# First attention of a fused eight-layer kernel: a head's query and key weights absorbed two heads ahead instead of one

## The reference, cut to what matters

```python
q = rmsnorm(x @ Wq_a) @ Wq_b             # rank 192, then per head 128 plain + 64 rotary columns
ckv = x @ Wkv_a                          # 64 compressed + 64 rotary columns
kv = rmsnorm(ckv[..., :64]) @ Wkv_b      # per head 128 key + 128 value columns
scores = (q_nope @ k_nope.T + rope(q_pe) @ rope(k_pe).T) * 192 ** -0.5
probs = softmax(where(causal, scores, -inf))
out = concat_heads(probs @ v) @ Wo
```

## Time and profile before

| what | us |
|---|---|
| median of 3 runs | 3092.81 |
| lowest, highest run | 3090.31, 3095.83 |
| profiled execution: its span | 3095.1 |
| profiled execution: its own time outside the span | not given |
| PE busy in the span | 2679.5 (87%) |
| DVE, ACT, POOL busy | 1575.6, 1260.3, 650.4 |
| the first attention's heads | from about 60 to 1127 |

### The profile page before, as it was taken

The page is one execution under the profiler, slowest core; times in us unless marked ns, Lnnn a source line. Parts: engine busy times, 40 slices in busy tenths (PEclk is TensorE's granted clock), DMA queues, the critical chain, the costliest instruction groups (busy, mean ns, idle before and its releaser), DMA issues. The chain is left out here.

```text
span 3095.1 us, 37611 instructions
## 1 busy us (share of the span) xinstructions
PE 2679.5 (87%) x12992; PEld 1314.1 (42%) x12992; DVE 1575.6 (51%) x2697; ACT 1260.3 (41%) x1756; POOL 650.4 (21%) x506
## 2 busy tenths in 40 slices
PE   4999999999999989664999997568999998799766
PEld 3455555555555557222333332322333333344344
DVE  3444544545445434456777774526777773111343
ACT  3344444444444432220666566222565665100321
POOL 0344444444444430230000001210000001000121
PEclk7798898998989889886999998789999999899878
DMA  2010110100111021021000000141011000300001
GB/s 61 13 36 26 31 37 26 36 26 26 36 33 34 22 72 62 20 76 49 14 14 21 20 1 15 41 106 37 22 25 39 22 1 14 110 0 0 16 0 51
DMA packets 72234, 99.82 MB, mean 32 GB/s; under 512 B 34536, under 2 KB 42984, under 8 KB 69824
## 3 DMA queue, kind: packets, MB, share of 16 engines
q1 hardware_dynamic: 72128, 98.31, 11.2%
HBM read 77.17 MB, written 20.84 MB: 32 GB/s over the span
## 5 line engine op out<-in xcount | busy, mean ns | idle before, releaser
L1935 POOL TENSOR_TENSOR l0a_p_low<-yT,l0a_p_high 128x1024 fp32r<-128x1024 f32 (+7 forms) x256 | 396.4, 1554 | 569.4 <-ACT l0a_p_high L1997 568.9
L1431 DVE TENSOR_REDUCE l2a_mx<-ps 128x1 f32<-128x512 f32 x512 | 338.2, 689 | 125.0 <-PE ps L1272 123.7
L1431 DVE TENSOR_REDUCE l1a_mx<-ps 128x1 f32<-128x512 f32 x512 | 337.3, 689 | 114.2 <-PE ps L1272 112.3
L1398 ACT ACTIVATE l1a_prob<-ps 128x1024 f32<-128x1024 f32 x256 | 250.7, 1019 | 131.3 <-PE ps L1311 93.6
L1398 ACT ACTIVATE l2a_prob<-ps 128x1024 f32<-128x1024 f32 x256 | 250.4, 1019 | 131.4 <-PE ps L1311 93.8
L2050 DVE TENSOR_REDUCE l0a_mx<-ps 128x1 f32<-128x512 f32 (+3 forms) x384 | 202.6, 551 | 187.8 <-PE ps L1847 185.9
L1984 ACT ACTIVATE yT<-ps 128x1024 f32<-128x1024 f32 (+7 forms) x256 | 166.1, 649 | 314.9 <-PE ps L1867 215.8
L1272 PE MATMUL ps<-l1a_k,l1a_q 96*128 96x512 bf16 x512 | 200.4, 401 | 65.3 <-DMA l1a_k<-l1a_k_parts 48.4
L173 POOL TENSOR_TENSOR applied<-prepared,neghalf 128x2 f32<-128x2 f32 x64 | 58.3, 911 | 903.0 <-DVE prepared L154 903.0
L1272 PE MATMUL ps<-l2a_k,l2a_q 96*128 96x512 bf16 x512 | 192.0, 389 | 46.7 <-DMA l2a_k<-l2a_k_parts 33.7
L1997 ACT CAST l0a_p_high<-yT 128x1024 fp32r<-128x1024 f32 (+7 forms) x256 | 172.3, 673 | 7.1
(11 more groups left out here) (286 smaller groups left out, 4494.3 us busy)
## 6 DMA issues: line engine op xcount, KB each, us to landing
l0a_woh<-in_l0a_wo SPq DMA_DIRECT2D x32, 256.0 KB, 2.7
l0a_cos_recip<-l0a_recip_row SPq DMA_DIRECT2D x32, 256.0 KB, 3.7
l0a_o<-l0a_o_pair SPq DMA_DIRECT2D x16, 512.0 KB, 2.7
yT<-l0a_o SPq DMA_DIRECT2D x16, 512.0 KB, 3.3
l0a_wqnT<-in_l0a_wqnT SPq DMA_DIRECT2D x32, 96.0 KB, 2.9
l1a_q_parts<-l1a_part SPq DMA_DIRECT2D x12, 256.0 KB
l1a_q<-l1a_q_parts SPq DMA_DIRECT2D x8, 384.0 KB
l2a_q_parts<-l2a_part SPq DMA_DIRECT2D x12, 256.0 KB
```

Source lines behind the costliest of these rows:

```text
L1398: nc.scalar.activation(prob[:, s % (2 * GROUP), :], ST[s % 2].rearrange("p b n -> p (b n)"), ACT.Exp, scale=SCALE).then_inc(s_exp, 1)
L1431: nc.vector.tensor_reduce(mx[:, m // NT, m % NT, c:c + 1], MB[c], AX.X, ALU.max).then_inc((s_red0, s_red1)[c], 1)
L1935: nc.gpsimd.tensor_tensor(p_low[:, j % 4, P * j:T], prob[:, j % 4, P * j:T], p_high[:, j % 4, P * j:T], ALU.subtract).then_inc(s_pl, 1)
```

## The change

On PE job 0 leaves the head's border. It is done for head h + 2 in step j = 4 of head h, behind job 16. On ACT `ready` of stage 0 for head h + 2 follows the cast of tile 4. On DVE the two subtractions become `absorbed_rest`, called for the next head but one behind the row of maxima. Before the first head job 0 is done for heads 0 and 1. The last three heads are written out, since heads 30 and 31 have no head after next: the loops have one turn less.

```diff
@@ PE @@
-            def head(h, par, next_turn, first, last):
+            def head(h, par, next_turn, first, last, turn_after=None):
                 for j in range(NT):
-                    if j == 0 and not last:
-                        job(h + 1, 1 - par, next_turn, 0, False)
                     if j == 0 and not first:
                         pv(h - 1, NT - 1)
...
                         for k in range(*PLAN[j][1:3]):
                             job(h + 1, 1 - par, next_turn, k, False)
+                    if j == 4 and turn_after is not None:
+                        job(h + 2, par, turn_after, 0, False)
...
+            job(1, 1, 0, 0, False)
             scores(0, 0, 0)
             scores(0, 0, 1)
-            head(0, 0, 0, True, False)
-            with pe.Fori(0, NH // 2 - 1) as i:
-                head(i * 2 + 1, 1, i + 1, False, False)
-                head(i * 2 + 2, 0, i + 1, False, False)
+            head(0, 0, 0, True, False, 1)
+            with pe.Fori(0, NH // 2 - 2) as i:
+                head(i * 2 + 1, 1, i + 1, False, False, i + 1)
+                head(i * 2 + 2, 0, i + 1, False, False, i + 2)
+            head(NH - 3, 1, NH // 2 - 1, False, False, NH // 2 - 1)
+            head(NH - 2, 0, NH // 2 - 1, False, False)
             head(NH - 1, 1, None, False, True)
@@ ACT @@
-                    if j == 0 and not last:
-                        ready(h + 1, 1 - par, next_pair, 0)
...
                     if j and not last:
                         ready(h + 1, 1 - par, next_pair, j)
+                    if j == 4 and absorb:
+                        ready(h + 2, par, None, 0)
...
+            ready(1, 1, None, 0)
             head(0, 0, 0, True, False)
@@ DVE @@
-            def prepare(h, par, done=None, first=False):
-
-
+            def absorbed_rest(h, par):
                 for k, rows in enumerate((P, 64)):
                     dve.wait_ge(s_wh, h * 2 + k + 1)
                     nc.vector.tensor_tensor(wh_low[0:rows, par, k, :], wh[0:rows, par, k, :],
                                             wh_high[0:rows, par, k, :], ALU.subtract).then_inc(s_wl, 1)
+
+            def prepare(h, par, done=None, first=False, absorb=True):
...
                                         ALU.mult).then_inc(s_mrow, 1)
+                if absorb:
+                    absorbed_rest(h + 1, 1 - par)
...
+            absorbed_rest(0, 0)
             prepare(0, 0, first=True)
```

More of the change, by code:

```diff
@@ L1976, in cast, with head @@
                 nc.scalar.copy(q_high[:, par, 512 * c:512 * c + 512], q32[:, 512 * c:512 * c + 512]).then_inc(s_high, 1)
-            def head(h, par, next_pair, first, last, second=False):
+            def head(h, par, next_pair, first, last, second=False, absorb=True):
                 for j in range(NT):
@@ L2014, in _ @@
             head(2, 0, 1, False, False)
-            with act.Fori(1, NH // 2 - 1) as i:
+            with act.Fori(1, NH // 2 - 2) as i:
                 head(i * 2 + 1, 1, i + 1, False, False)
                 head(i * 2 + 2, 0, i + 1, False, False)
-            head(NH - 1, 1, None, False, True)
+            head(NH - 3, 1, NH // 2 - 1, False, False)
+            head(NH - 2, 0, NH // 2 - 1, False, False, absorb=False)
+            head(NH - 1, 1, None, False, True, absorb=False)
             act.wait_ge(s_on, NH - 1)
@@ L2087, in _ @@
             finish(1, 1, 0)
-            with dve.Fori(1, NH // 2 - 1) as i:
+            with dve.Fori(1, NH // 2 - 2) as i:
                 prepare(i * 2 + 2, 0, i * 2)
@@ L2092, in _ @@
                 finish(i * 2 + 1, 1, i)
+            prepare(NH - 2, 0, NH - 4)
+            finish(NH - 4, 0, NH // 2 - 2)
+            prepare(NH - 1, 1, NH - 3, absorb=False)
+            finish(NH - 3, 1, NH // 2 - 2)
             for h in (NH - 2, NH - 1):
```

## The result

The changed kernel takes 3209.48 us (median; 3204.77 to 3222.17) against 3092.57 for the kernel before: ratio 1.0385, 95% interval 1.0361 to 1.0409, some 117 us more. The forecast was 3169, 76 more, in a range up to 3222. The hold of PE (the time per head in which it stands and waits for ACT) came as worked out; the clock's part was twice as large.

A forecast was written before the change was run, and what follows sets the result against it. PE was taken to set the pace in the first attention's head loop. The span of 3095.1 us plus 39.3 of hold and 37 of clock (76), less 2.3 from span to median, gave 3169 us, range 3120 to 3222.

The forecast's parts named there:

- ACT's queue order holds PE: Sixth tile: its exponential queues behind copies and casts awaiting late products; PE held 1.45 us, net 1.31 per head, 39.3 us.
- the wait at the row of maxima: After tile 8's scores and a PV: PE's 0.14 us wait per head goes, as DVE finishes while PE is held.
- Nothing gained at the head's border: Head's border: ACT's chain starts 0.8 us sooner, but PE does not wait for it there; no gain.
- DVE, POOL, SyncE, start and end at nothing: Delayed subtractions, unmoved loads and heads written out of the loop cost nothing; start and end at most 2 us.
- The clock: Behind the fifth tile: the thin stretch of products and hold brings PE's clock down, adding 37 us.
- the shortest kind: Behind the fifth tile: low-clock stretch of 3.1 us costing 1.37 us, taken in 27 heads, 37 us.
- clock down for longer: Rival, chance 0.10: each head takes a middle low stretch too, 94 us beside 39 of hold, 3226 us.
- Hold without clock: Rival, chance 0.18: PE is held at the sixth tile's exponential, but the clock stays as before, 3132 us.
- middle low stretch: Behind the fifth tile: 7.1 us at the lower clock, costing 3.1 us, or 94 us in 30 heads as upper bound.
- The rival in which the clock wins: Rival, chance 0.07: products leaving the border make the lower clock rarer; at best all 72 us return, 3060 us.

The follow-up runs named there:

- e1: Changed kernel with ACT's copies and casts of the absorbed weights one tile later, behind the sixth tile's cast: 3054.5 us, ratio 0.9874 to the kernel before.
- e6: e1 plus one unread matmul of 256 columns per head behind the moved products: 3092.63 us, ratio 0.9985 to the kernel before.
- e8: e1 with the projection's matmuls ordered by rows, 128-row ones first, then 64-row ones: 2966.81 us, ratio 0.9569 to the kernel before.
- e3: Changed kernel with seven unread matmuls of 384 columns behind the moved products, filling the hold: 3121.77 us, ratio 1.0069 to the kernel before.
- e5: Kernel before, nothing moved; ACT waits for the transpose L1851, then makes six unread casts (long artificial hold): 3246.24 us, ratio 1.0471.
- e9: Changed kernel with one unread matmul of 256 columns more per head behind the third tile: 3205.78 us, ratio 1.0355 to the kernel before.
- e10: Changed kernel with three unread matmuls of 256 columns more per head behind the third tile: 3168.45 us, ratio 1.0235 to the kernel before.
- e2: Kernel before, nothing moved; ACT waits for the transpose L1851, then makes two unread casts (short artificial hold): 3129.27 us, ratio 1.0093.
- e7: Changed kernel with the projection's matmuls ordered by rows, 128-row ones first, then 64-row ones: 3075.17 us, ratio 0.9804 to the kernel before.
- e4: Kernel before with the projection's matmuls ordered by rows, the three of 128 rows before the three of 64: 2980.61 us, ratio 0.9625.

## Why the prediction was right, and what was mis-sized

*ACT's queue order holds PE.* Right at each step: the exponential started 0.75 us behind the copy, and from the start of L1812 to the scores of tile 8 it took 450.61 - 448.60 = 2.01 us, against 1.97 worked out; PE stood for 1.32 us of it, 30 times, and the wait at the row of maxima went. Net 1.28 us per head against 1.31, 38.4 us against 39.3. (In the earlier trace rows the clock goes down at 533.7, not 533.8; nothing hangs on it.) The full-clock head I put at 31.3 took 31.30. e1 shows it from the other side: with the wait behind the sixth cast the hold is gone.

*Nothing gained at the head's border.* Right in this kernel and in e6. It is true only while PE does not wait for anything there; in e8, where the projection is short, the sooner ACT is worth some 0.2 us per head.

*DVE, POOL, SyncE, start and end at nothing.* Right within the numbers: inside the heads PE's only other wait is one of 0.8 us in all for DVE, and outside the 30 heads the span is 3208.2 - 1086.31 = 2121.9 us against 3095.1 - 972.96 = 2122.1.

*The clock.* Mechanism right (e3, e5), size wrong, and this is the step that missed: "I take the shortest kind in nine heads of ten, 27 x 1.37 = 37 us". The term measured 74.9 us. The short kind costs 1.5 us (32.8 against 31.30), close to 1.37, but it came in 13 heads only, 19 us, and not in 27. Three heads had the clock low from behind the fifth tile into the next head, at 43.5 - 31.3 = 12.3 us each, 37 us, a kind that stood in no row of before and in no rival; it runs over the place behind the projection too, and what part of the 12.3 us was lost there already cannot be told apart. The rest is the older place: stretches behind the projection cost about 91 us in 24 heads instead of 72 in 23, as all 24 lasted 10.2 us, where 13 of the 23 did before. I priced the new dip as if it stood alone, where a low clock can also last until the next one. That the time still lies inside the range is in part luck and the width of the range: 3209 is nearer to the 3226 of the rival "clock down for longer" than to 3169, and in three kernels with the same hold (this one, e9 and e10) the clock cost between 20 and 75 us more than before.

*The rivals.* Hold without clock describes e2 and e3, not this kernel. Clock down for longer had the size nearly right, but not the picture: not a middle low stretch in each head, but 13 short ones and three very long ones. The rival in which the clock wins had its point: e1, without the hold, lost 44 us less to the clock than the kernel before. It lost here because the hold brought a second dip.

The Trainium skill, "TensorE: Matmul & The Clock Gate", section "A second HAM failure mode: psum-queue depth-cycling", says that small idle moments between groups of matmuls make the clock swing; the 16 low stretches behind a hold of 1.32 us agree. By the Trainium skill's section "Why this matters for your kernels" in the same page, a gap this short would have been harmless; that fits the 1.0 us of e2, and the 16 low stretches here and the 25 of e5 say that it does not hold for 1.3 and 1.8.

## What to carry to other kernels

When a producer's work is moved, move its consumer's place in the other engine's queue by the same measure of time, not by the same loop index: a wait put ahead of work that was ready four microseconds early takes that cover away. Price an idle moment of PE in a dense loop by its own length and, where the clock may fall behind it, by up to about twice that again (75 us beside 38 of hold here, 100 beside 54 in e5, about nothing beside 29 in e2); filling it with unread matmuls tells the two apart. Before judging an edit that changes a loop's length by tenths of a microsecond, remove what makes the clock swing (here matmuls that alternate between 128 and 64 rows), or vary the length on purpose, and take more than two runs.

## What the runs showed of the hardware that I had not expected

A loop in which the clock swings can have a time that changes with its length out of all proportion: one matmul of 0.12 us more per head cost 38 us (e1 to e6). 0.36 more seemed to gain about 40 (changed kernel to e10), but with two runs 28 us apart this is less sure, and the five runs of e7 are 66 us apart at one length. Low stretches behind the fifth tile lasted 3.4 us in 13 heads of the changed kernel and 30.7 in three. And alternating matmuls of 128 and 64 rows cost 0.43 us each for 512 columns at full clock, where grouped ones cost 0.23 to 0.35: in the grouped order the weight load of a matmul with the same row count as the one before starts 0.23 or 0.24 us ahead of it, while that one still runs, and at a change of row count only together with it (425.88 and 425.88 in e4). The Trainium skill, "TensorE: Matmul & The Clock Gate", section "The mechanism", says that a weight load overlaps a running matmul only when the row groups differ, and, just before, that it is also pulled ahead when it goes to the background weight buffer. Here the steps are shortest when the row groups are the same, so the first rule does not describe this case, and the measurement decides; the 64-row operands lie in the first 64 of the same 128 rows, and groups that share no row were not tried.
